# Moving the multiply of the token-shift mix and the ReLU of the key projection from VectorE to ScalarE

## What is computed

```python
x = x + _layernorm(attn(_layernorm(x), Wq, bq, Wk, bk, Wv, bv))
x = x + _layernorm(ffn(_layernorm(x), W_r, W_k, W_v, mu_r, mu_k))

def ffn(x, W_r, W_k, W_v, mu_r, mu_k):
    x_prev = concatenate([zeros, x[:, :-1, :]], axis=1)   # the token before
    xr = mu_r * x + (1.0 - mu_r) * x_prev
    xk = mu_k * x + (1.0 - mu_k) * x_prev
    r = sigmoid(einsum('btc,dc->btd', xr, W_r))
    k = einsum('btc,dc->btd', xk, W_k)
    k_act = square(relu(k))
    return r * einsum('btc,dc->btd', k_act, W_v)
```

## Time and profile before

| | us |
|---|---|
| median of 2 timed runs | 5365.67 (5288.56 and 5442.78) |
| the profiled execution | 5270.37 |
| its span on the slowest core (core 7) | 5268.6 |
| spans of the 8 cores | 5250.6 to 5268.6 |
| busy on that core: PE, ACT, DVE | 3181.5 (60%), 2052.5 (39%), 1840.0 (35%) |
| mean granted TensorE clock of the 8 cores | 0.714 to 0.718 |

### The profile page before, as it was taken

One profiled execution on the slowest core, in us unless ns is written; L12 is line 12 of the kernel. 1 busy time (PEld: TensorE's weight loads), 2 busy tenths in 40 slices (PEclk: granted clock), 3 DMA queues, 4 the chain that ended last, 5 costly groups with the idle time before them and its releaser, 6 DMA issues.

```text
span 5268.6 us, 51432 instructions; the slowest of 8 cores (5250.6 to 5268.6 us)
## 1 busy us (share of the span) xinstructions
PE 3181.5 (60%) x15744; PEld 1312.9 (25%) x15744; DVE 1840.0 (35%) x3790; ACT 2052.5 (39%) x2953; POOL 23.8 (0%) x32
## 2 busy tenths in 40 slices
PE   2976665194297666519439766642943976664293
PEld 1422222032142222114214222211411422221141
DVE  3113223644411323364440132236344023323635
ACT  3144554321415455432231544543223154454323
POOL 0000000000000000000000000000000000000000
PEclk9976666597597666559759756655976976665597
DMA  4210000313410000021431000012143100001213
GB/s 105 32 17 1 1 1 25 96 32 78 138 33 17 1 1 1 28 92 33 91 125 32 17 1 1 1 38 82 33 101 115 32 17 1 1 1 40 80 33 112
DMA packets 76271, 221.50 MB, mean 42 GB/s; under 512 B 10465, under 2 KB 10465, under 8 KB 76002
## 3 DMA queue, kind: packets, MB, share of 16 engines
q1 hardware_dynamic: 50978, 167.88, 9.5%
q0 software_dynamic: 25024, 50.33, 5.9%
HBM read 201.41 MB, written 67.11 MB: 51 GB/s over the span
## 4 chain that ended last, share of the span: by engine, by line
PE 44%; DVE 25%; ACT 18%; issue 8%; DMA 3%; DVEq 1%; SPq 1%; ACTq 1%
ACT S L464 13%; PE psA L509 9%; PE psB L305 8%; PE psA L305 8%; DVE S L588 6%; PE psB L452 5%; DVE S L561 3%; PE psA L796 2%; DMA out<-POOL 2%; PE psA L347 2%; PE psB L796 2%; PE psB L347 2%; DVE S L702 2%; DVE S L735 1%; DVE S L485 1%
## 5 line engine op out<-in xcount | busy, mean ns | idle before, releaser
L509 PE MATMUL psA<-S 128*65 128x512 bf16 (+4 forms) x3328 | 1004.0, 397 | 264.8 <-ACT S L464 170.8
L464 ACT ACTIVATE S<-psB 128x1024 bf16<-128x1024 f32 x896 | 918.1, 1025 | 347.6 <-PE psB L452 297.3
L452 PE MATMUL psB<-S 64*128 64x512 bf16 (+3 forms) x2560 | 591.8, 458 | 390.8 <-DVE S L588 381.8
L485 DVE TENSOR_TENSOR S<-S,CB 128x128 bf16<-128x128 bf16 x1024 | 230.7, 225 | 1326.4 <-ACT S L473 1016.4
L305 PE MATMUL psA<-S,W 128*128 128x512 bf16 x2048 | 483.9, 394 | 71.1 <-DVE S L739 71.1
L509 PEld LDWEIGHTS psA<-S 128*65 128x65 bf16 x3328 | 322.1, 135 | 786.9 <-issue 778.4
L305 PE MATMUL psB<-S,W 128*128 128x512 bf16 x2048 | 458.0, 382 | 0.0
L469 ACT ACTIVATE S<-psB 128x128 bf16<-128x128 f32 (+2 forms) x384 | 147.8, 385 | 773.7 <-PE psB L452 760.9
L225 ACT ACTIVATE S<-S 128x1024 bf16<-128x1024 bf16 (+1 forms) x192 | 203.0, 1058 | 474.9 <-DVE S L819 375.1
L561 DVE CAST S<-psA 65x2048 bf16<-65x2048 f32 x64 | 146.4, 2287 | 646.0 <-PE psA L509 612.1
L452 PEld LDWEIGHTS psB<-S 64*128 64x128 bf16 x2560 | 132.7, 98 | 849.2 <-issue 834.0
(11 more groups left out here) (97 smaller groups left out, 2812.2 us busy)
## 6 DMA issues: line engine op xcount, KB each, us to landing
S<-x SPq DMA_DIRECT2D x96, 512.0 KB, 4.2
POOL<-x SPq DMA_DIRECT2D x32, 512.0 KB, 5.5
yscr<-POOL SPq DMA_DIRECT2D x32, 512.0 KB, 2.6
yscr<-S SPq DMA_DIRECT2D x32, 512.0 KB, 2.9
POOL<-yscr SPq DMA_DIRECT2D x32, 512.0 KB, 7.4
S<-yscr SPq DMA_DIRECT2D x32, 512.0 KB, 6.5
out<-POOL SPq DMA_DIRECT2D x32, 512.0 KB, 4.2
out<-S SPq DMA_DIRECT2D x32, 512.0 KB, 4.1
```

Of the source, the lines that this page charges most:

```text
L452: blk["tS"] = E("tensor", lambda e, slot=slot, ki=ki, c0=c0, c1=c1, ch=ch, rb=rb: e.matmul(psB[:, 512 * slot:512 * slot + (c1 - c0)], S3[r ...
L464: t_exp = E("scalar", lambda e, slotA=slotA, half=half: e.activation(PT(half)[:, 0:1024], psB[:, 512 * slotA:512 * slotA + 1024], AF.Exp, ...
L485: tm = E("vector", lambda e, half=half, c0=c0, dlo=dlo, e2=e2: e.tensor_tensor(PT(half)[:, 512 * e2 + dlo - c0:512 * e2 + dlo - c0 + 128], ...
L509: last_pv = E("tensor", lambda e, ki=ki, h=h, e2=e2, cs=cs, ce=ce, half=half, c0=c0, fb=fb, lb=lb, qlo=qlo: e.matmul(psA[0:65, QW * e2 + ( ...
```

## The change

In the mix, the multiply into tmp moves from VectorE to ScalarE (an Identity activation with a scale per partition). It now multiplies by 1 - mu, and the scalar_tensor_tensor, still on VectorE, multiplies the unshifted z by mu and adds the shifted tmp. tmp has two buffers, taken in turn: the ScalarE instruction of a chunk waits for the scalar_tensor_tensor of two chunks before, and the scalar_tensor_tensor waits for the ScalarE instruction of its chunk. The 16 ScalarE instructions (8 for xr, 8 for xk) stand in ScalarE's stream at the place of the mix, ahead of the r projection's Tanhs. In `evac_k` the clip with its scale becomes a ScalarE Relu activation with a scale; the Square after it, the two buffers and the freeing of PSUM after the first of the two stay.

```diff
-            tmp = POOL[:, 0:1024].bitcast(BF16)
             dst_toks = {}
             xr_cc_toks = []
+            tmp_state = [[], []]
+            ci = 0
             for (dst, mucol, omcol) in ((S2, C_MUR, C_OMR), (S3, C_MUK, C_OMK)):
                 tmix = None
                 for cc in range(CC):
                     lo = S * cc
-                    w = []
+                    tb = ci % 2
+                    ci += 1
+                    tmp = POOL[:, 1024 * tb:1024 * tb + 1024].bitcast(BF16)
+                    w = list(tmp_state[tb])
                     if cc == 0 and dst is S2:
-                        w = ([zT_tok, prev_attn_P_done] + pool_state[0]
-                             + pool_state[1] + pool_state[2] + ywrites_done)
-                    E("vector", lambda e, lo=lo, mucol=mucol, cc=cc: e.tensor_scalar(
-                        tmp[:, 0:S], S1[:, lo:lo + S],
-                        CONST[:, mucol + cc:mucol + cc + 1], None, ALU.mult),
-                        waits=w, inc="V")
-                    E("vector", lambda e, lo=lo, dst=dst, omcol=omcol, cc=cc: e.scalar_tensor_tensor(
-                        dst[:, lo + 1:lo + S], S1[:, lo:lo + S - 1],
-                        CONST[:, omcol + cc:omcol + cc + 1],
-                        tmp[:, 1:S], ALU.mult, ALU.add), inc="V")
+                        w += ([zT_tok, prev_attn_P_done] + pool_state[0]
+                              + pool_state[1] + pool_state[2] + ywrites_done)
+                    ttmp = E("scalar", lambda e, lo=lo, omcol=omcol, cc=cc, tmp=tmp: e.activation(
+                        tmp[:, 0:S], S1[:, lo:lo + S], AF.Identity,
+                        scale=CONST[:, omcol + cc:omcol + cc + 1]),
+                        waits=w, inc="A")
+                    tst = E("vector", lambda e, lo=lo, dst=dst, mucol=mucol, cc=cc, tmp=tmp: e.scalar_tensor_tensor(
+                        dst[:, lo + 1:lo + S], S1[:, lo + 1:lo + S],
+                        CONST[:, mucol + cc:mucol + cc + 1],
+                        tmp[:, 0:S - 1], ALU.mult, ALU.add),
+                        waits=[ttmp], inc="V")
                     tmix = E("vector", lambda e, lo=lo, dst=dst, mucol=mucol, cc=cc: e.tensor_scalar(
                         dst[:, lo:lo + 1], S1[:, lo:lo + 1],
                         CONST[:, mucol + cc:mucol + cc + 1], None, ALU.mult),
                         inc="V")
+                    tmp_state[tb] = [tst]
...
-                tkr = E("vector", lambda e, ps=ps, krelu=krelu: e.tensor_scalar(
-                    krelu[:, 0:S], ps[:, 0:S], 0.0, 0.70710678118654755,
-                    ALU.max, ALU.mult),
+                tkr = E("scalar", lambda e, ps=ps, krelu=krelu: e.activation(
+                    krelu[:, 0:S], ps[:, 0:S], AF.Relu, scale=0.70710678118654755),
                     waits=[ptok] + krelu_state[kb] + (p4_attn_reads[-3:] if dj < 2 else []),
-                    inc="V")
+                    inc="A")
```

## The result

| | before | changed |
|---|---|---|
| timed runs: median (lowest to highest) | 5288.56 (5263.13 to 5477.36), 23 runs | 5328.29 (5290.19 to 5565.06), 24 runs |
| the profiled execution | 5270.37 | 5297.54 |
| spans of its 8 cores, mean | 5257.3 | 5285.0 |
| ratio changed / before, 95% interval | | 1.0047 (1.0026 to 1.0069) |

The change makes the kernel slower by about 25 to 30 us, half a per cent: within the 2%, but clear of no change. The 5365.67 us that stood as the time before was the middle of two runs, 5288.56 and 5442.78. It was no yardstick for 5310 us: by it my forecast reads as a gain, by the profiled execution from which it was worked out it is a loss.

A forecast was written before the change was run, and what follows sets the result against it. VectorE was taken to bound the xr mix, TensorE what follows. Terms 7.52 + 2.85 - 0.47 = 9.90 us a sequence, four of them 39.6, gave 5270.4 + 39.6 = 5310 us; 8-in-10 range 5275 to 5460.

The forecast's parts named there:

- Part 1: xr mix: VectorE's chunk falls from 3.65 to 2.78 us, ScalarE's multiply takes 2.00; dj = 1 ends 4.74 us sooner.
- the faster VectorE: Mix: rival that scalar_tensor_tensor gets faster with its new operands, +0.6 us a sequence, 5273 us; chance 3%.
- the mutual slowing: Mix: rival that VectorE and ScalarE slow each other on SBUF, +15 us, 5325 us; chance 8%.
- Part 2: r projection: xk multiplies ahead of first Tanh idle TensorE 12.3 us before dj = 2, losing 7.52 us a sequence.
- The rival by which the Tanh is not held back: r projection: ScalarE reaches the first Tanh as early as before, gaining 5.21 us a sequence, 5250 us; chance 5%.
- Part 3: r projection, dj = 2: TensorE's lower clock behind the new idle time costs 2.85 us a sequence.
- Part 4: End of k projection: Relu on ScalarE instead of VectorE's clip shortens the idle time, -0.47 us a sequence.

The follow-up runs named there:

- the reordered kernel: Changed kernel with the 8 xk multiplies placed behind the r projection's Tanhs in the streams; ratio 0.9943 to the kernel before, die mean -25.9 us.
- only the Relu: Kernel before with only the k projection's clip moved from VectorE to a ScalarE Relu; ratio 0.9961, die mean -10.2 us.
- only the mix: Changed kernel with the k projection's clip put back on VectorE; ratio 1.0053 to the kernel before, die mean +31.7 us.
- only the wait: Kernel before with the r projection's first Tanh also waiting for xk chunk 3 on VectorE, nothing moved; ratio 1.0073, die mean +31.6 us.
- more matmuls: Kernel before with 8 matmuls more a sequence at the start of the k projection; ratio 0.9993, die mean -2.5 us.

## Why the prediction was right and wrong

| per sequence, us | forecast | measured |
|---|---|---|
| xr mix and start of dj = 2 | +7.52 | +7.4 |
| clock behind the new idle time | +2.85 | +2.1 |
| Relu on ScalarE, idle time ahead of the v projection | -0.47 | -0.68 |
| v projection | 0 | -1.96 |
| sum | 9.90 | 6.9 |

(The measured +7.4 is 29.6 / 4 from the six cores with complete matmul records; the clock's is what is left of 35.4 / 4 = 8.85 without the lines above and below it.)

**Part 1 held.** The multiply takes 2.00 us (2001 to 2002 ns in all 64) and VectorE's chunk 2.78 us. L739 kept its 2350 ns beside a streaming ScalarE, so neither the faster VectorE nor the mutual slowing of the rivals is there.

**Part 2 held**, to 0.1 us: 12.34 us of idle TensorE (core 0) against 12.3 forecast. Two experiments settle the mechanism. A wait without any moved work makes the same stall, and the moved work without its place in front of the Tanh turns 29.8 us of loss into 25.9 us of gain. So ScalarE is not the wrong engine for these instructions; the program order was. The rival by which the Tanh is not held back describes the reordered kernel in direction and roughly in size: forecast -20.8 us, measured -25.9. Its sum, too, has nothing for the v projection; how much of the other 5 us lies there the trace of that kernel can't tell, with its longer spans.

The table load cost 1.28 us behind a busy ScalarE too: the multiply ends at 1076.80, the load starts at 1076.88, and the Tanh at 1078.17, as its end says. The 1.38 us for a drain that the Trainium skill gives in "ScalarE: Activation LUTs" (section "What ACT_TABLE_LOAD costs") are not seen here, and the measurement decides.

**Part 3's term was mis-sized**: 2.1 us where I took 2.85 from the v projection's rows. The clock stood at its lower level for 4.5 us of the 15 us from the start of dj = 2 (mean over the 8 cores and 4 sequences), which at half the rate loses 2.2 us.

**Part 4 held in direction.** Relu takes 1877 ns from PSUM against VectorE's 2292, and the steps between the engines cost 0.2 us less than I had them. The rule in the Trainium skill's "ScalarE: Activation LUTs" (section "Rules for kernel authors") that relu belongs on VectorE fails for this form. No table load came with Relu.

**The step that failed is one that the sum does not have.** I put the change of the v projection at nothing, without a reason: I took it as it was in the kernel before, 9.50 to 9.96 us for its first chunk, and even used these rows as the price of any idle time. They were no price of an idle time of 4.85 us. They were what that idle time costs at the moment at which it fell before: the clock fell 2.7 to 4.1 us into it, in 31 of 32 places with over 0.8 us of it still to come, and stayed low for long. Each kernel that shifts something ahead of it, by a stall or even by added matmuls, or ends it sooner, by a shorter evacuation, loses less there. In the changed kernel no place is left on the costly side:

| kernel | idle ahead of the v projection, us | falls with over 0.8 us of it to come, of 32 | low time, us | v projection, us a sequence against before |
|---|---|---|---|---|
| before | 4.85 | 31 | 13.4 | 0 |
| changed | 4.17 | 0 | 7.0 | -1.96 |
| only the Relu | 4.17 | 10 | 7.9 | -2.07 |
| only the mix | 4.85 | 14 | 8.8 | -1.42 |
| only the wait | 4.85 | 8 | 7.0 | -2.41 |
| more matmuls | 4.85 | 12 | 5.6 | -2.56 |

The last two columns don't go in step with the third, since the low time also counts the falls further on in the v projection, which differ from kernel to kernel, and the part of the low time in which TensorE is idle costs nothing.

So 8 us of the forecast's 39.6 were given back in a stage that the diff does not touch, the other lines took off 4 more, and 27.6 are left, the difference between the mean spans of the two profiled executions (5285.0 - 5257.3, before rounding). The forecast ratio of 1.0075 lies just above the interval. The difference is within the 2%, as forecast, and 5310 us is 0.2% above the changed kernel's profiled 5297.54.

**What fixes the moment.** The four sequences and eight cores start at different times, and yet in the kernel before the fall comes within the same 1.4 us in all of them. The clock's record ties it to the last rise, which comes soon behind the xr mix, at the start of the dense matmuls. From that rise to the fall it is 105.8 us in all 32 places of before and in all 32 with only the Relu moved. It is 99.0 us in all 96 of the changed kernel, only the mix and only the wait, where the stall puts the last rise into dj = 2. With more matmuls it is 109.2 us in 20 places and 105.8 in 12, the two groups of falls above. What the edits change is how much work lies between that rise and the idle time. Why the times from rise to fall are these, no run here shows.

## What to carry to other kernels

When an instruction is moved to an engine with little to do, look at what stands behind it in that engine's stream: here eight multiplies for the next projection delayed one short Tanh, and with it a PSUM half that TensorE was waiting for. Issue work that is needed late behind the evacuations that are needed now. And take no price for a clock loss from one place, nor from the length of an idle time alone: compare it over several kernels or sequences whose timing differs, or the effect of an edit may be the effect of a shift.

## What the runs showed of the hardware that I had not expected

- Behind the same idle time of 4.85 us the same 32 matmuls took 9.3 to 10.0 us in 31 of 32 places of one kernel, and 8.6 to 9.2 us in another that had done more work. What decided it was whether the clock fell with over or under about 0.8 us of idle time still to come: 6.8 or 3.4 us at the lower level at first, in all 192 places. 8 added matmuls a sequence made the kernel no slower (-2.5 us by the die mean).
- Two edits gave -10.2 and +31.7 us alone and +29.8 together; the clock makes the parts of a change interact, though they touch different stages.
- With bursts of 4 matmuls every 2.46 us, 0.5 to 1.4 us of idle ahead of each, the clock rose to its full level within the mix in all 32 places; with one every 2.78 us it did in none.
